# Attention times values in twos: eight groups of column products gathered into four in a cross-attention block

## The reference

```python
xq  = layer_norm(x, qn_w, qn_b)
ctx = layer_norm(context, cn_w, cn_b)
q = (xq @ q_w).reshape(B, N, H, D)
k, v = split((ctx @ kv_w).reshape(B, M, 2, H, D))
attn = einsum('bnhd,bmhd->bhnm', q, k) * D ** -0.5
attn = softmax(where(xa_mask, -max, attn), axis=-1)
out  = einsum('bhnm,bmhd->bnhd', attn, v).reshape(B, N, C)
x = x + out @ proj_w + proj_b
h = layer_norm(x, n2_w, n2_b)
return x + gelu(h @ fc1_w + fc1_b) @ fc2_w + fc2_b
```

## Time and profile before

| | us |
|---|---|
| median of 3 runs | 812.7 (811.55 to 813.7) |
| profiled execution, device time | 810.04 |
| its span in the trace | 808.2 |
| TensorE matmuls busy | 772.6 |
| VectorE busy | 616.3 |
| ScalarE busy | 560.1 |
| GpSimd busy | 180.1 |
| mean granted TensorE clock | 0.975 of full speed |

### The profile page before, as it was taken

One profiled execution on the slowest core, in us unless ns is written; L12 is line 12 of the kernel. 1 busy time (PEld: TensorE's weight loads), 2 busy tenths in 40 slices (PEclk: granted clock), 3 DMA queues, 4 the chain that ended last, 5 costly groups with the idle time before them and its releaser, 6 DMA issues.

```text
span 808.2 us, 16998 instructions
## 1 busy us (share of the span) xinstructions
PE 772.6 (96%) x5615; PEld 632.7 (78%) x5615; DVE 616.3 (76%) x1379; ACT 560.1 (69%) x781; POOL 180.1 (22%) x185
## 2 busy tenths in 40 slices
PE   5748999999999999999999999999999999999998
PEld 5635769788787978878797978879797887869687
DVE  6736778698787879878787887878787887878453
ACT  4617776778777677777677777767767777776832
POOL 2311122222202222220222222021222212121230
PEclk8659999999999999999999999999999999999999
DMA  8877659394775939385684938567493956739100
GB/s 238 155 112 148 76 152 144 115 142 111 145 120 142 128 116 147 102 163 104 153 115 139 131 109 154 106 150 109 139 141 124 139 118 136 106 110 149 32 28 26
DMA packets 89478, 100.47 MB, mean 124 GB/s; under 512 B 9060, under 2 KB 63576, under 8 KB 89432
## 3 DMA queue, kind: packets, MB, share of 16 engines
q1 hardware_dynamic: 88694, 99.55, 64.5%
q10 hardware_dynamic: 754, 0.53, 0.3%
HBM read 69.22 MB, written 30.83 MB: 124 GB/s over the span
## 4 chain that ended last, share of the span: by engine, by line
PE 73%; issue 10%; DMA 6%; ACT 4%; DVE 3%; POOL 2%; ACTq 0%; SPq 0%; DVEq 0%; POOLq 0%
PE A L866 20%; PE F L866 12%; PE ST L936 8%; PE A L945 7%; PE F L990 7%; PE F L992 6%; PE F L991 6%; PE ST L918 3%; DMA QM<-sd 2%; PE A L961 2%; DMA xin<-in_x 2%; PE A L918 1%; DMA raw_q<-in_L_xattn_q_w 1%; ACT QM L528 1%; DMA sd<-cT_lo 1%
## 5 line engine op out<-in xcount | busy, mean ns | idle before, releaser
L508 ACT ACTIVATE probs<-ST 78x512 f32<-78x512 f32 x256 | 137.3, 588 | 50.2 <-PE ST L936 48.3
L990 PE MATMUL F<-w_hi,g_hi 128*128 128x256 f32 x480 | 141.8, 295 | 0.0
L992 PE MATMUL F<-w_hi,g_lo 128*128 128x256 f32 x480 | 133.9, 279 | 0.0
L991 PE MATMUL F<-w_lo,g_hi 128*128 128x256 f32 x480 | 133.9, 279 | 0.0
L594 DVE TENSOR_TENSOR g_lo<-g_f,g_hi 128x512 fp32r<-128x512 f32 x128 | 107.1, 837 | 32.9 <-ACT g_hi L542 30.2
L528 ACT ACTIVATE QM<-mask_u 77x2048 fp32r<-77x2048 uint8 x64 | 116.9, 1898 | 0.0
L423 POOL TENSOR_TENSOR xin<-xin,projb 128x1024 f32<-128x1024 f32 x16 | 38.2, 2388 | 314.7 <-DMA xin<-in_x 314.7
L990 PEld LDWEIGHTS F<-w_hi,g_hi 128*128 128x128 f32 x480 | 90.3, 188 | 18.6 <-issue 18.5
L936 PE MATMUL ST<-QM,KM 127*78 127x256 f32 x512 | 93.5, 294 | 3.0 <-ACT probs L508 0.7
L434 POOL TENSOR_TENSOR oT_lo<-g_f,oT_hi 128x512 fp32r<-128x512 f32 x32 | 41.2, 1287 | 234.8 <-ACT oT_hi L515 234.8
L936 PEld LDWEIGHTS ST<-QM,KM 127*78 127x78 f32 x512 | 59.8, 146 | 40.3 <-ACT probs L508 33.3
(11 more groups left out here) (168 smaller groups left out, 1843.5 us busy)
## 6 DMA issues: line engine op xcount, KB each, us to landing
QM<-qd SPq DMA_DIRECT2D x48, 512.0 KB, 14.6
xa<-in_x SPq DMA_DIRECT2D x16, 512.0 KB, 4.0
qd<-q_hi SPq DMA_DIRECT2D x32, 256.0 KB, 2.2
qd<-q_lo SPq DMA_DIRECT2D x32, 256.0 KB, 2.3
xin<-in_x SPq DMA_DIRECT2D x16, 512.0 KB, 5.0
QR<-qd SPq DMA_DIRECT2D x16, 480.0 KB, 5.2
out<-xin SPq DMA_DIRECT2D x30, 256.0 KB, 6.8
KM<-kd SPq DMA_DIRECT2D x48, 156.0 KB, 7.0
```

Source lines behind the costliest of these rows:

```text
L508: act.activation(probs[:, quad % NSLOT, 2 * (p % 2):2 * (p % 2) + 2], ST[p % 2][0:MX].rearrange("p (h n) -> p h n", n=N), ACT.Exp, scale=S ...
L990: pe.matmul(dst, g_hi[:, k, tok], w2_hi[:, k], start=(k == 0), stop=False)
L991: pe.matmul(dst, g_hi[:, k, tok], w2_lo[:, k], start=False, stop=False)
L992: last = pe.matmul(dst, g_lo[:, k, tok], w2_hi[:, k], start=False, stop=(k == HC - 1))
```

## The change

Only TensorE's order inside `body` changes. Every call stays. Quads 0 and 1, 2 and 3, 4 and 5, 6 and 7 are issued side by side. `q_proj(j+1, 0)` and its wait come ahead of `attend(j, 0)` and of the wait for the last gelu. `attend(j, 1)`, `attend(j, 3)` and `attend(j, 5)` move ahead of the two scores that stood before them. The fc2 groups 3 to 7 of the first token tile are gathered between the scores and the attends. The waits for xT_lo, k_lo and q_lo stay ahead of the attends with quads 2, 4 and 6.

```diff
@@ -1072,44 +1072,42 @@
                     k_proj(j + 1)
                 scores(j, 4)
                 scores(j, 5)
+                if prep:
+                    q_proj(j + 1, 0)
                 pe.wait_ge(gelu_done, HC * j)
                 attend(j, 0)
-                if prep:
-                    q_proj(j + 1, 0)
+                attend(j, 1)
                 scores(j, 6)
                 scores(j, 7)
-                attend(j, 1)
                 if prep:
                     q_proj(j + 1, 1)
                 scores(j, 8)
                 scores(j, 9)
+                if mlp and prep:
+                    fc2(j - 1, 0, 3)
                 if prep:
                     pe.wait_ge(xT_lo_done, KC * (j + 2))
                 attend(j, 2)
+                attend(j, 3)
                 scores(j, 10)
                 scores(j, 11)
                 if mlp and prep:
-                    fc2(j - 1, 0, 3)
-                attend(j, 3)
+                    fc2(j - 1, 0, 4)
+                    fc2(j - 1, 0, 5)
                 scores(j, 12)
                 scores(j, 13)
-                if mlp and prep:
-                    fc2(j - 1, 0, 4)
                 if prep:
                     pe.wait_ge(k_lo_done, G * (j + 2))
                 attend(j, 4)
+                attend(j, 5)
                 scores(j, 14)
                 scores(j, 15)
-                attend(j, 5)
-                if mlp and prep:
-                    fc2(j - 1, 0, 5)
                 if mlp:
                     fc2(j - 1, 0, 6)
+                    fc2(j - 1, 0, 7)
                 if prep:
                     pe.wait_ge(q_lo_done, G * (j + 1) + 1)
                 attend(j, 6)
-                if mlp:
-                    fc2(j - 1, 0, 7)
                 attend(j, 7)
                 if mlp:
                     for k in range(HC):
```

## The result

The changed kernel takes 806.35 us (median of 9 runs, 805.27 to 810.2) against 812.36 us for the kernel before in the same rounds. The ratio is 0.9934, 95% interval 0.9919 to 0.9950, so 5.4 us less (4.1 to 6.6). The forecast was 6 us less, 806.7 us.

A forecast was written before the change was run, and what follows sets the result against it. TensorE, busy 96% of the span, was taken to bound the kernel. The terms -4.95 + 1.35 - 0.3 - 2.0 + 0.15 = -5.75, rounded to -6, took the 812.7 us median to 806.7 us, range 802.5 to 812.0.

The forecast's parts named there:

- Part 2: Between scores 8 and project(j, 1): three of four merges become a wait on oT_lo, some 0.9 us a pair; gain 0.3.
- Part 1: At the attends: moving one next to another saves 0.30 to 0.37 us, taken as 0.33; 18.5 us of TensorE time.
- Part 3: q_proj(j+1, 0) ahead of attend: waits 0.27 us on xT_lo in five pairs, cost 1.35 us, up to 2.0.
- Part 4: Scores in fours in pair 15: the last attend comes 0.15 us later; cost 0.15, bounds 0 and 1.2.
- Part 5: Ahead of the transposes of h: VectorE runs early, gaining 0.15 us in 13 pairs, 2.0 us, bounds 0 and 2.6.
- A: At project(j, 1): no wait, the whole TensorE time arrives, 18.8 us less, 794 us; chance 0.11.
- B: Nothing measurable: xT_lo waits 0.27 or more in all pairs, VectorE not ahead before h; about 811.7 us; chance 0.15.
- C: Behind the new wait ahead of project(j, 1): the granted clock falls, dense products run slower, about 828 us; chance 0.06.

## Why the prediction was right, point by point

**What arrives and what doesn't (Part 2): right.** It was the step on which all hung. The stretch from scores 8 to the second project was 13.83 us a pair before and is 13.83 after; 0.3 us of gain in it were expected and none came. The two waits grew by 12.3 us in 14 pairs, 0.88 a pair, for 0.9 forecast. The rear merges alone show it, and the pair of runs with the statistics moved shows the cause: take the statistics out of VectorE's chain and the whole change is worth 12.7 - 1.7 = 11 us.

**The price of a merge (Part 1): right.** The second attend stands 0.46 behind the first in two halves of one bank too, as in rows 4 for two banks. A merge behind scores 8 takes off 0.30, where 0.30 to 0.33 was used. The first merge gave 0.28 in the stretch from scores 4 to scores 8 with q_proj ahead and 0.32 with q_proj behind. Add the 0.09 that the late load costs to the 0.28, and it is the 0.37 of the upper bound.

**q_proj ahead (Part 3): right for five pairs, too low for the nine others.** Five waits on xT_lo, 1.2 us in all, for 1.35 forecast. In the nine others I allowed 0 to 0.05 of waiting and took 0. No matmul waits there, but the first weight load does, at 0.09 a pair and 0.8 us in all, so the whole cost is the 2.0 of the upper bound. The five pairs gain next to nothing. From scores 0 to scores 8 the trace has 2.8 us less over 14 pairs, for 4.6 - 1.35 = 3.3.

**Scores in fours (Part 4): fits, not shown.** Pair 15 takes 52.02 us to the end where it took 51.83, 0.19 more for 0.15. But in the kernel before with only the statistics moved, whose program for pair 15 is the old one, it takes 52.12, so traces differ by more than the term. The upper bound of 1.2 is out.

**VectorE gets ahead (Part 5): right in kind, size 1.4 for 2.0.** The addition no longer holds, and the transposes of h follow the last fc2 matmul in one step, changed kernel, pair 7:

```profile
412.26 0.28 PE L992 MATMUL F<-w_hi,g_lo 128*128 128x256 f32 x1
412.38 0.71 PE L961 MATMUL A<-ident,o_tok 128*128 128x128 f32 x5
```

From the second project to there it is 7.78 us a pair instead of 7.88, 1.4 us in all; the steps into the transposes held 1.6 us beyond the ordinary ones and hold none now. (The working counts 12 steps for a product of 12 matmuls; it has 11, and was complete at 407.8. Nothing hangs on it.)

**The sum.** The terms as measured, 2.8 + 1.4 in pairs 1 to 14 (652.5 us before, 648.3 after), 0.6 in pair 0 and -0.2 in pair 15, make 4.6 us. The first pair starts 0.7 us later in the trace of after, so the spans differ by 3.9. The medians say 5.4 and 4.3. The forecast 5.75 carried 0.5 us too much at q_proj, 0.6 at h and 0.3 of slack, and 0.2 too little in pair 0. So the mechanism was right, and that 806.7 lies 0.35 us from the median is luck: the trace gives a microsecond less than the forecast, and the two sets of runs differ by as much.

**The rivals.** A (all of it arrives, 794) is out for this kernel. With the statistics moved most of it does arrive, 11 us of the 18.8. B (nothing measurable) is out: VectorE did get ahead before h, and waits of 0.27 on xT_lo in all pairs did not come, though q_proj's load meets xT_lo in all of them. C (the clock falls behind the hole) is out: the granted clock is 1.00 in every stretch shown, with holes of up to a microsecond.

**What stays open.** The first merge alone gave 1.5 and 2.8 us in its two forms where its traces have 2.7 and 4.5 in the stretch it touches. In pairs 1 to 14 about 1 us of it comes back in each trace, mostly ahead of the maxima and the next scores; the rest of the difference lies in pairs 0 and 15 and in the scatter. Whether the loads give back so much on average was not separated from scatter.

## What to carry to other kernels

Ahead of counting what an edit takes off the busiest engine, find the next point at which that engine meets another chain, and split the edit there: what is saved ahead of the chain's own start moves the chain along, what is saved behind it turns into a wait. If such a chain holds work that nobody waits for (here statistics for a later pair), moving that out and shortening the busy engine are worth more together than apart, here 12.7 us against 1.7 and 5. Size a wait from more than one execution before building on it, and where it is a wait for a load, look whether the load is slow or issued late.

## What the runs showed of the hardware

Eight 32-column matmuls between full-width ones cost 0.76 us of TensorE time, behind another such group 0.46, in one bank or two. The Trainium skill (TensorEngine Tiling (Array Packing), Key Properties) says that changing the tiling mode drains the engine and changing only the tile doesn't; the trace agrees, with about 0.1 us on either side.

Not expected: what a late weight load costs. Where q_proj's first load starts 0.11 us ahead of its matmul, the second matmul comes 0.23 to 0.24 behind the first; where the load starts 0 to 0.04 ahead of it, behind xT_lo or behind an attend, it comes 0.30 to 0.35 behind. From the load to the second matmul it is 0.33 to 0.36 in either case.

Nor was it expected where the gather of q comes late. It is waited for 0.1 us in all in pairs 1 to 14 of before, and in two pairs of the kernel before with only the statistics moved:

```profile
PE ST L918 <- DMA QR<-qd: 1.3, 2, 0.7
```

The gather itself is steady: 5.7 to 6.3 us from its first issue to its last landing, in pairs 1 to 14 of every trace here. What differs is its issue, 4.9 to 8.2 us behind scores 8. SyncE issues in the order of its program, and the store of the low part of q, which the gather needs, stands there behind the gather of k. In pair 3 of that kernel, one of the two pairs, VectorE and SyncE:

```profile
205.22 0.75 DVE L651 SCALAR_TENSOR_TENSOR q_lo<-F,bias,q_hi 128x512 fp32r<-128x512 f32 x1 [0.67 <-ACT q_hi L497]
...
206.97 0.43 SPq L248 DMA_DIRECT2D KR<-kd  x1
...
207.91 0.43 SPq L305 DMA_DIRECT2D qd<-q_lo  x1
210.24 0.32 SPq L309 DMA_DIRECT2D QR<-qd  x1
```

The low part is ready at 205.97 and its store is issued at 207.91. In pair 7 of the same run it is issued 0.60 us behind the low part and nothing waits. An order of SyncE with that store ahead of the gather of k was not tried.
